# A stem phase that ends without waiting for its stores, with nine constants loaded later and text gathers spread over three phases

## The reference, cut to what matters

```python
# image branch: 32 images, 3 x 96 x 96
h = leaky_relu(batchnorm(conv2d(x, stem_w, stem_b, 4)))      # 96 channels, 24 x 24 pixels
offset = conv2d(h, off_w, off_b, 4)                          # 32 x 6 x 6: where to sample
h = deform_conv(h, offset, dcn_w, dcn_b)                     # 16 taps, bilinear, 192 channels
h = leaky_relu(batchnorm(h))                                 # 36 visual tokens of 192
# text branch: 32 x 128 tokens
t = fake_quant_lastdim(weight)[x_txt]                        # rows of 192, 8 bit per row
h = jnp.concatenate([h, t], axis=1)                          # 164 tokens per image
h = h + attention(layernorm(h))                              # 12 heads of 16, window 64 each way
h = h + kan_layer(kan_layer(layernorm(h), w1), w2)           # splines, 192 -> 512 -> 192
```

## Time and profile before

| | us |
|---|---|
| runs | 2505.47, 2510.21 (median), 2511.16 |
| profiled execution, whole | 2506.58 |
| its span, first to last instruction | 2504.9 |
| TensorE busy | 2310.6 (92%) |
| VectorE busy | 1896.7 (76%) |
| ScalarE busy | 1407.2 (56%) |
| GpSimd busy | 230.2 (9%) |
| stem ends, offset begins | at 70.2 |
| offset ends, sample begins | at 93.8 |

### The profile page before, as it was taken

One profiled execution on the slowest core, in us unless ns is written; L12 is line 12 of the kernel. 1 busy time (PEld: TensorE's weight loads), 2 busy tenths in 40 slices (PEclk: granted clock), 3 DMA queues, 4 the chain that ended last, 5 costly groups with the idle time before them and its releaser, 6 DMA issues.

```text
span 2504.9 us, 49398 instructions
## 1 busy us (share of the span) xinstructions
PE 2310.6 (92%) x20297; PEld 2159.9 (86%) x20297; DVE 1896.7 (76%) x2364; ACT 1407.2 (56%) x1391; POOL 230.2 (9%) x132
## 2 busy tenths in 40 slices
PE   6599959999999936999999999989999999999999
PEld 6266848777777726999999999989999999999999
DVE  6699754566666518675766767569999999999995
ACT  5488213344444425544435353478888888888881
POOL 4322000000000003121211112000000000000000
PEclk9799966899999967999999999999999999999999
DMA  8456230111111110000000000130000000000000
GB/s 245 126 151 152 63 141 21 41 44 42 41 43 43 36 33 9 26 19 25 19 20 21 18 25 15 34 124 23 22 22 22 24 26 24 22 22 22 22 18 10
DMA packets 99472, 116.33 MB, mean 46 GB/s; under 512 B 15287, under 2 KB 90567, under 8 KB 98631
## 3 DMA queue, kind: packets, MB, share of 16 engines
q1 hardware_dynamic: 81155, 93.36, 12.4%
q0 software_dynamic: 3616, 10.54, 1.7%
q10 hardware_dynamic: 14596, 10.83, 1.5%
HBM read 83.83 MB, written 30.86 MB: 46 GB/s over the span
## 4 chain that ended last, share of the span: by engine, by line
PE 61%; DVE 1%; issue 1%; DMA 0%; POOL 0%; ACT 0%; SPq 0%; POOLq 0%; DVEq 0%
PE spline_acc L1820 26%; PE spline_acc L1793 9%; PE spline_acc L1792 9%; PE spline_acc L1794 9%; PE spline_acc L1814 5%; PE spline_acc L1816 2%; PE spline_xT L1773 0%; DMA spline_x<-h_scr 0%; DVE spline_weights_low L1475 0%; DVE spline_xn L677 0%; DVE spline_f L1513 0%; DVE spline_t L1496 0%; DVE spline_b L1491 0%; DVE spline_b L1485 0%; DVE spline_a L1480 0%
## 5 line engine op out<-in xcount | busy, mean ns | idle before, releaser
L1820 PE MATMUL spline_acc<-spline_weights,spline_f 128*128 128x192 f32 x3936 | 672.0, 328 | 0.0
L1820 PEld LDWEIGHTS spline_acc<-spline_weights,spline_f 128*128 128x128 f32 x3936 | 637.2, 190 | 0.0
L1792 PE MATMUL spline_acc<-spline_f,spline_weights_high 128*128 128x328 f32 x1536 | 479.8, 312 | 7.2 <-DVE spline_f L1513 7.2
L1793 PE MATMUL spline_acc<-spline_f,spline_weights_high 128*128 128x328 f32 x1536 | 482.6, 314 | 0.0
L1794 PE MATMUL spline_acc<-spline_f,spline_weights_low 128*128 128x328 f32 x1536 | 476.3, 310 | 0.0
L1513 DVE SCALAR_TENSOR_TENSOR spline_f<-spline_n,spline_a 128x984 fp32r<-128x984 f32 x128 | 151.1, 1180 | 200.0 <-PE spline_acc L1794 198.3
L1792 PEld LDWEIGHTS spline_acc<-spline_f,spline_weights_high 128*128 128x128 f32 x1536 | 290.1, 189 | 7.4 <-issue 7.4
L1793 PEld LDWEIGHTS spline_acc<-spline_f,spline_weights_high 128*128 128x128 f32 x1536 | 289.1, 188 | 0.0
L1794 PEld LDWEIGHTS spline_acc<-spline_f,spline_weights_low 128*128 128x128 f32 x1536 | 288.8, 188 | 0.0
L1524 DVE SCALAR_TENSOR_TENSOR spline_f<-spline_n,spline_b 128x1536 f32<-128x1536 f32 x164 | 286.9, 1749 | 0.0
L1814 PE MATMUL spline_acc<-spline_weights_split,spline_f_high 128*128 128x384 f32 x656 | 218.2, 389 | 8.2 <-issue 8.2
(11 more groups left out here) (197 smaller groups left out, 3978.9 us busy)
## 6 DMA issues: line engine op xcount, KB each, us to landing
sample_pos<-pos_scr SPq DMA_DIRECT2D x32, 540.0 KB, 4.3
hid_scr<-spline_hid SPq DMA_DIRECT2D x64, 164.0 KB, 1.8
spline_xn<-hid_scr SPq DMA_DIRECT2D x41, 256.0 KB, 3.1
attend_spread<-rec_scr SPq DMA_DIRECT2D x128, 61.5 KB, 2.2
pix_scr<-stem_by_pixel SPq DMA_DIRECT2D x32, 225.0 KB, 4.9
sample_h<-pix_scr POOLq DMA_DIRECT2D x32, 225.0 KB, 4.4
spline_weights_raw<-w SPq DMA_DIRECT2D x1, 6144.0 KB, 20.2
spline_weights<-w SPq DMA_DIRECT2D x4, 1536.0 KB, 6.2
```

The costliest lines, as they stand in the source:

```text
L1792: nc.tensor.matmul(z, high, x_high, start=start, stop=False)
L1793: nc.tensor.matmul(z, high, x_low, start=False, stop=False)
L1820: last = nc.tensor.matmul(z, f_rest[i][:, cols], w2[:, i, r, :], start=False, stop=stop)
```

## The change

Three things. The wait for the 32 stores goes from the stem's end to the offset phase's end, beside the wait for the positions; for that the buffers `by_pixel` and their semaphores now live over both phases. SyncE issues one constant after each of the first five pairs instead of two after each of the first seven; the other nine are issued by ScalarE at the start of the offset phase, and VectorE's list there has `text.form` ahead of the work on the attention constants instead of behind it. The 32 gathers are split 12, 12 and 8: twelve in the stem, twelve in offset, and eight in sample between GpSimd's first two loads and its loop.

```diff
     PIECES = 3
+    FIRST = 5
...
-        self.attend_count = 16 * (len(self.loads) - 5)
+        self.attend_count = 16 * (len(self.loads) - self.FIRST)
...
     GROUP = 4
+    PACED = 12
...
             for p in range(PAIRS - RING):
                 turn(p // RING, p % RING)
-                for dst, src, done in c.loads[2 * p:2 * p + 2]:
+                for dst, src, done in c.loads[p:p + 1] if p < c.FIRST else ():
                     sp.dma_start(dst, src).then_inc(done, 16)
             for u in range(RING):
                 results_out(PAIRS - RING + u, u)
-            for u in range(RING):
-                sp.wait_ge(pixel_out[u], 32 * (PAIRS // RING))
...
-            for p in range(PAIRS):
+            for p in range(text.PACED):
                 pool.wait_ge(pix_done, 2 * p + 2)
                 text.gather(pool, p)
...
+            for u in range(RING):
+                sp.wait_ge(pixel_out[u], 32 * (PAIRS // RING))
             sp.wait_ge(pos_out, 16 * NG)
...
         def _(act):
+            for dst, src, done in c.loads[c.FIRST:]:
+                act.dma_start(dst, src).then_inc(done, 16)
             act.wait_ge(c.attend_in, c.attend_count)
...
-            for b in range(PAIRS, B):
+            for b in range(text.PACED, 2 * text.PACED):
                 text.gather(pool, b)
...
+            for n in chunks:
+                text.form(nc, dve, n)
             dve.wait_ge(ones_set, 2)
             nc.vector.tensor_copy(c.xe[D1:P, :], c.ones_row[D1:P, :]).then_inc(attend_ready, 1)
             dve.wait_ge(c.attend_in, c.attend_count)
...
-            for n in chunks:
-                text.form(nc, dve, n)
             dve.wait_ge(conv_done, 1)
...
             for u in range(2):
                 load(u, u)
+            for b in range(2 * text.PACED, B):
+                text.gather(pool, b)
             with pool.Fori(1, B // 2) as t:
```

More of the change, by code:

```diff
@@ L44 @@
 PATCH = 3 * TAPS
+RING = 4
 ROWC = 5
@@ L218, in fold_norms, with stem_phase @@
     s.run(nc.vector.tensor_tensor(shift, shift, beta, ALU.add))
-def stem_phase(nc, c, patches, stem_w, vec_in, ident_in, inv, shift, hT_all, pix_scr, text, txt_idx):
-    RING = 4
+def stem_phase(nc, c, patches, stem_w, vec_in, ident_in, inv, shift, hT_all, by_pixel, pixel_out, pix_scr, text, txt_idx):
     UP = P // 2
@@ L237, in stem_phase @@
         pix = ps("by_pixel", [P, 2, 512])
-        by_pixel = [sb(f"stem_by_pixel{u}", [P, 2, NPIXC * C1]) for u in range(RING)]
         vectors_in = sem("vectors_in")
@@ L247, in stem_phase @@
         chan_ready, pix_ready = sem("stem_chan_ready"), sem("stem_pix_ready")
-        pixel_out = [sem(f"stem_pixel_out{u}") for u in range(RING)]
         block = stack.enter_context(nc.Block())
@@ L386, in _, with offset_phase @@
                     pair(t, u)
-def offset_phase(nc, c, inv, shift, hT_all, pos_scr, text, chunks):
+def offset_phase(nc, c, inv, shift, hT_all, pixel_out, pos_scr, text, chunks):
     GI = 8
@@ L1871, in tokens @@
             c.stage(nc, stack, a)
-            hT_all = memories(nc, stack)[0]("stem_by_channel", [P, B * PIX])
-            stem_phase(nc, c, a["patches"], a["stem_w"], a["norm_vec"], a["identity"], inv, shift, hT_all, pix_scr,
-                       text, a["txt_idx"])
-            offset_phase(nc, c, inv, shift, hT_all, pos_scr, text, (0,))
+            sb, ps, sem = memories(nc, stack)
+            hT_all = sb("stem_by_channel", [P, B * PIX])
+            by_pixel = [sb(f"stem_by_pixel{u}", [P, 2, NPIXC * C1]) for u in range(RING)]
+            pixel_out = [sem(f"stem_pixel_out{u}") for u in range(RING)]
+            stem_phase(nc, c, a["patches"], a["stem_w"], a["norm_vec"], a["identity"], inv, shift, hT_all,
+                       by_pixel, pixel_out, pix_scr, text, a["txt_idx"])
+            offset_phase(nc, c, inv, shift, hT_all, pixel_out, pos_scr, text, (0,))
         with ExitStack() as stack:
```

## The result

| | before | after |
|---|---|---|
| median of five runs each, us | 2510.21 | 2489.44 |
| ratio, with its 95% interval | | 0.9906 (0.9885 to 0.9927) |
| profiled execution, whole | 2506.58 | 2486.14 |
| its span | 2504.9 | 2484.4 |

The account below looks back on a forecast made before the run. TensorE was busy 92% of the span, but the first three phases counted, with GpSimd's gathers ending the stem: -4.7 (stem), -2.3 (offset), +0.3 (sample) made -6.7 us, forecast 2502 us, between 2499.9 and 2503.5; range 2488 to 2509.

Parts of the forecast that it names:

- Who ends the stem, and what the wait is worth: Stem's end: GpSimd's last gather, not SyncE's store wait, delays offset; removing the wait alone is worth nothing.
- Step 1: Stem: with nine constants gone VectorE ends at 52.0 instead of 65.36, 13.4 us earlier.
- Step 2: Stem: fourth gather held to VectorE's end, eight gathers follow, offset begins at 65.5 instead of 70.2: -4.7 us.
- rival 1: Stem: GpSimd keeps up and SyncE is last, offset begins at 52.9; in all -19.3 us, 2487 to 2491; chance 0.25.
- The sum of -6.7: Stem, offset and sample together: -4.7, -2.3 and +0.3 us.
- Step 4: Offset: with twelve gathers SyncE becomes last and the phase takes 21.3 us instead of 23.6: -2.3 us.
- Step 5: Offset: constants arrive 9.2 to 11.6 us after its start, VectorE's work on them hidden by the convolution: nothing.
- rival 2: Offset: late constants delay L474 by 2.6 us; with a DMA-bound stem no gain is left, 2506 to 2510; chance 0.20.
- Step 6: Sample: eight gathers beside the first positions cost +0.3 us, at most 0.6; third image load has ten microseconds of cover.
- Rival 3: Sample: held gathers make an image load late, three long holds giving +9.7 us, 2516 to 2520; chance 0.05.

Follow-up runs that it names:

- The wait alone: Kernel before with only the store wait moved from the stem's end to offset's end, gathers and constants as before: 2499.26 us, ratio 0.9995.
- the kernel with the loads first: Changed kernel with the nine constant loads issued by ScalarE at the stem's start instead of in offset: 2482.7 us, ratio 0.9921 to the kernel before.
- the one with the longer rest: Kernel with five unpaced gathers at the stem's start, TensorE also held before offset's convolution until the attention constants are there: 2491.25 us, 0.9951.
- the five-gather version: Changed kernel with gathers split into five unpaced at the stem's start, 12 in offset, 5 in sample, 10 in deform: 2484.69 us, later one time of 2473.41.
- The rests: Five gathers at the stem's start, TensorE held before offset's convolution until text's first chunk is quantised (2482.59 us) or also the attention constants are there (2491.25).
- The spread version: Changed kernel with gathers 5 unpaced in the stem, 12 in offset, 8 at sample's start, 7 between image loads: 2481.91 us, again 2482.47.

## Why the prediction was right and wrong

**Who ends the stem, and what the wait is worth: right.** The wait alone gave nothing, and it counts 1.8 us (2.95 - 1.13) once no gather is last.

**Step 1, VectorE's end at 52.0: right.** 51.4 to 53.8 us in all profiles in which the nine constants had left the stem and VectorE had no gap put in.

**Step 2, "I expect the fourth held again from about 20 us": this is the step that failed.** In the compared profile the stem gave -13.5 us and not -4.7. The mechanism and its price are right; that it would come each time, and so early, is not. Of the seven profiles in which twelve or sixteen paced gathers met a dense stem, three have the fourth held to the stem's end (32.83, 32.83 and 32.75 us; two of them start offset at 65.7 and 65.0, forecast 65.5), and four don't: the changed kernel in its first two (longest gathers 13.04 and 2.6 us), the kernel with the loads first (13.03) and that without gathers in offset (8.08). I had seen a gather of 1.07 us in an unbroken run and put 0.25 on rival 1 for it; the rows of one execution could not tell how often. What a hold costs is 65 less 55, some 10 us in the eight gathers and GpSimd's way to the barrier. The sum of -6.7 is what the changed kernel shows when the fourth is held; not held, the stem alone gives 13.5 to 15.2, and the median lies nearer to that.

Which gather is held goes, in the traces, with the moment at which it starts. In the twelve profiles with paced gathers and no gap put in, eleven gathers started 0.23 to 0.26 us after the start of the first of a pair's two by-channel ReLUs, and all eleven were held, for 5.6 to 32.8 us. Thirty-six started 0.42 to 0.60 us after one, and none took over 1.2 us. Of five that started at 0.33 two were held. All sixteen gathers of over 3 us, eight of them in the middle of the stem, ended 0.8 us after VectorE had stopped. So a few tenths of a microsecond in its start go with what a gather costs, and one program can give both. No run set this moment on purpose; it is a reading of the traces.

The Trainium skill's rule (SBUF — State Buffer, Who interferes with whom), that a VectorE instruction with two SBUF inputs blocks a GpSimd instruction that reads SBUF until it has finished, agrees with the gathers of 1.6 us (0.95 and one ReLU of 0.65 to 0.75). Those of 2.1 to 2.6 outlast two ReLUs, and those of 3.3 to 33 a whole run of them.

**Step 4, offset's length: right in kind, and hidden in the profile first compared.** Without the crawl, with the constants in time and twelve gathers or none beside it, it was 20.4 to 21.9 us (forecast 21.3). In the compared profile the crawl made it 28.2.

**Step 5, the constants cost nothing: right in the compared profile** (11.5 us). In nine other profiles they came 10.9 to 13.9 us after the start, beyond the forecast's 9.2 to 11.6 in six of them, and cost 0.3 us at most. In four they came at 14.6 to 15.4: in one the crawl hid it, in the one with the longer rest TensorE waited for them, and in two it cost 2.2 and 2.7 us, rival 2's mechanism at its price of 2.6; it never ate the whole gain, since the stem was not bound by DMA beside it.

**Step 6:** eight gathers in sample; two were held 4.83 us, and the third image load was still in time. The changed kernel's sample was 1.2 us longer, 0.1 shorter and 0.3 longer in its three profiles (forecast +0.3). Rival 3 was not seen.

**What no step had.** (1) The crawl: +7.8 us in offset with the change, +11.7 in the kernel before. It was in none of the twelve profiles from three chips, in all six from two others, and in the first comparison in the changed kernel's profile and not in the other's. The program doesn't decide it (the five-gather version has it once and once not), and the traffic doesn't make it. It begins each time after the first 65 to 75 of the 128 matmuls. Whether it needs the gathers beside it wasn't tried on a chip that had it; whether the chip decides or the moment, and what TensorE waits for, stays open. The rests that seemed to cure it were on a chip that never had it. (2) Attention's length. The kernel before has 588.4, 587.5 and 577.1 us, the changed one 576.0, 571.1 and 571.0, all other kernels 572 to 582. The 12.4 us of the profiled difference are not far from the 10.4 us that one program differed by on one chip. It is a matter of the time at the lower clock, as shown above: 117.4 us in the profile of before and 87.9 in that of after. But the two groups of three don't overlap, so that a part of it may be the change's; that is not settled.

In the compared profiles these errors partly cancel: against the forecast the stem gained 8.8 us more and attention 12.4 more, offset 6.9 less and sample 0.9 less. That the median fell inside the range, at its lower end, is in part luck.

What the medians say can be made to fit holds and crawls that come and go. They are -20.8 and -24.2 us on two chips, of which the second crawled in every profile; the starts of sample with a crawl before and after differ by 103.0 - 84.2 = 18.8 us, of profiles on three chips. On one without crawls the median is -17.3 us, where the three phases gain 6.7 in the held profile and, by the lengths measured in the others, would gain 14 to 19 without a hold. That sum is argued, not shown, and attention's length moves every time by up to 17 us beside it.

**A better version** was not shown. The spread version lies 2.1 us under the changed kernel on one chip and the five-gather version 2.1 us under it on another, and the intervals overlap in both cases. Both take away the hold. That this also takes away the slow times (to 2496.9 and 2501.6 in the changed kernel; to 2484.9 and 2485.8 beside them) isn't shown: the held execution that was profiled took 2482.26. Nor is one of the two better than the other. From offset's end to attention the spread one took 238.6 to 238.8 us in its two profiles and the five-gather one 237.2 and 239.6.

## What to carry to other kernels

A wait that shows two microseconds is worth them only if its engine is the last at the barrier: look at what it waits for in the barrier afterwards. Move a load out of a stretch in which DMA is full, to one where the engine that needs it still has other work, and reckon with a transfer a third slower than the best (here 11.0 and 14.6 us in two executions of one program). And before you put a large chance on a thing that depends on how two engines meet, ask for more than one profile: the longest stall in one execution may be absent in the next of the same program.

## What the runs showed of the hardware that was not expected

- GpSimd's indirect DMA can be held through 20 us and more of back-to-back two-input VectorE instructions, 32.8 us here, until VectorE pauses; a pause of 0.25 us per pair was enough (no gather over 2.5 us). Whether it was held went with the tenths of a microsecond at which it started within VectorE's instruction: all eleven at 0.23 to 0.26 us, none of thirty-six at 0.42 to 0.60.
- Where a gather was a stem's last work, the next phase began 2.6 to 3.6 us after it, of which the barrier alone takes 0.2.
- A row of identical matmuls with nothing to wait for can fall from 8 to about 1 a microsecond for 8 to 14 us, starting in groups about 0.7 us or a multiple of it apart. It does so at either level of the granted clock: at 1.00, 32 matmuls in 8 us where 64 belong, and at 0.55, 23 in 12.3 us.
- The clock granted in attention differed between two executions of one program on one chip, by 10 us of time (89.0 and 116.5 us at the lower level).
